# Identity products in TensorE's idle times, and a last stage that scatters its first picks ahead of its second picks

## What is computed

```python
h = _layernorm(x, g, b).reshape(Tn, D)
logits = h @ Wr
top_vals, top_idx = jax.lax.top_k(logits, TOP_K)          # 2 of 7
gates = jax.nn.softmax(top_vals, axis=-1)
idx = top_idx.T.reshape(-1)                               # all first picks, then all second picks
onehot = jax.nn.one_hot(idx, E_ROUTED, dtype=jnp.int32)
pos = jnp.sum(jnp.cumsum(onehot, axis=0) * onehot, axis=-1) - 1
keep = pos < CAPACITY
xe = zeros.at[idx, where(keep, pos, CAPACITY)].set(h[tok], mode='drop')
ye = (silu(xe @ W1) * (xe @ W3)) @ W2
routed = zeros.at[tok].add(ye[idx, pos] * gates * keep)
out = routed + silu(h @ W1s) * (h @ W3s) @ W2s
x = _layernorm(x + out)
```

## Time and profile before

| | us |
|---|---|
| median of 3 runs | 2411.19 |
| fastest, slowest | 2404.15, 2413.72 |
| the profiled execution | 2407.47 |
| its span, first to last instruction | 2405.6 |
| TensorE busy | 2038.5 (85%) |
| VectorE busy | 1331.8 (55%) |
| ScalarE busy | 1129.3 (47%) |
| GpSimd busy | 969.7 (40%) |
| mean granted TensorE clock | 0.906 |

### The profile page before, as it was taken

How to read it: one execution, slowest core, us unless ns; L and a number is a source line. 1 busy time by engine, 2 the same in 40 slices (tenths; PEclk the granted TensorE clock), 3 DMA queues, 4 the chain that set the end, 5 groups by cost and what they waited for, 6 DMA issues and landing times. The chain is left out here.

```text
span 2405.6 us, 59384 instructions
## 1 busy us (share of the span) xinstructions
PE 2038.5 (85%) x24530; PEld 1251.5 (52%) x24530; DVE 1331.8 (55%) x3370; ACT 1129.3 (47%) x2591; POOL 969.7 (40%) x868
## 2 busy tenths in 40 slices
PE   4988999869976899999999999999769756699773
PEld 2445666635543555565555555555535545355452
DVE  3545554447725776767776767776236423465322
ACT  1333445115523676767676767676415211145221
POOL 2010000011215887878787878787110133100123
PEclk8999999879968999999999999999769767889887
DMA  2110000000002021211111212121000032100411
GB/s 66 24 36 1 1 1 1 1 18 3 3 1 72 18 60 27 47 39 42 40 47 35 60 27 51 36 48 24 14 14 7 1 110 89 27 2 2 132 39 40
DMA packets 70558, 78.47 MB, mean 33 GB/s; under 512 B 10608, under 2 KB 48634, under 8 KB 70291
## 3 DMA queue, kind: packets, MB, share of 16 engines
q1 hardware_dynamic: 64098, 61.75, 9.9%
q0 software_dynamic: 3696, 10.56, 1.5%
q10 hardware_dynamic: 2496, 2.36, 0.4%
HBM read 40.90 MB, written 6.82 MB: 20 GB/s over the span
## 5 line engine op out<-in xcount | busy, mean ns | idle before, releaser
L3490 POOL TENSOR_TENSOR l1fb_rinv<-l1fb_ssq,neghalf 128x8 f32<-128x8 f32 x192 | 316.2, 1647 | 159.5 <-DVE l1fb_ssq L3533 157.0
L3633 ACT ACTIVATE l1fb_p<-ps,l1fb_shift 128x64 f32<-128x64 f32 x768 | 177.7, 315 | 158.7 <-PE ps L3789 137.8
L3492 POOL TENSOR_TENSOR l1fb_qk<-l1fb_qk,l1fb_r 128x512 f32<-128x512 f32 x192 | 244.5, 1273 | 0.0
L3696 PE MATMUL ps<-l1fb_wqkv,l1fb_xs 128*128 128x512 f32 x384 | 219.5, 655 | 10.3 <-DVE l1fb_r L3543 6.2
L3494 POOL TENSOR_TENSOR l1fb_qk<-l1fb_qk,l1fb_rinv 128x512 f32<-128x512 f32 x192 | 200.4, 1044 | 15.1
L3543 DVE TENSOR_TENSOR l1fb_r<-ps,l1fb_turn_tab 128x256 f32<-128x256 f32 x384 | 143.0, 414 | 0.0
L3540 DVE TENSOR_TENSOR l1fb_qk<-ps,l1fb_turn_tab 128x512 f32<-128x512 f32 x192 | 132.4, 690 | 14.4 <-POOL l1fb_qk L3492 12.5
L3531 DVE TENSOR_REDUCE l1fb_ssq<-l1fb_sq 128x8 f32<-128x512 f32 x192 | 129.8, 676 | 3.0 <-ACT l1fb_sq L3613 3.0
L3613 ACT ACTIVATE l1fb_sq<-ps 128x512 f32<-128x512 f32 x192 | 118.7, 618 | 11.9 <-PE ps L3696 11.2
L3727 PE MATMUL ps<-ident,l1fb_qk 128*128 128x128 f32 x768 | 116.6, 275 | 5.7 <-POOL l1fb_qk L3494 2.5
L3641 ACT ACTIVATE l1fb_both<-ps 128x512 f32<-128x512 f32 (+1 forms) x194 | 117.3, 605 | 8.3 <-PE ps L3789 7.7
(11 more groups left out here) (722 smaller groups left out, 4773.8 us busy)
## 6 DMA issues: line engine op xcount, KB each, us to landing
l1fb_v<-l1fb_v SPq DMA_DIRECT2D x48, 260.0 KB, 4.2
l1fb_v<-l1fb_v SPq DMA_DIRECT2D x48, 195.0 KB, 4.0
l1fb_wqkv<-in_L_ffn_Wqkv SPq DMA_DIRECT2D x24, 256.0 KB, 2.8
l3f_w<-in_L_ffn_W SPq DMA_DIRECT2D x21, 256.0 KB, 6.5
l1fb_wqkv<-in_L_ffn_Wqkv SPq DMA_DIRECT2D x6, 512.0 KB, 4.7
l1fb_wo<-in_L_ffn_Wo SPq DMA_DIRECT2D x6, 512.0 KB, 4.1
l1fb_w<-in_L_ffn_W SPq DMA_DIRECT2D x6, 341.0 KB, 3.0
l3f_xs<-zeros SPq DMA_DIRECT2D x1, 1344.0 KB, 6.9
```

The costliest lines, as they stand in the source:

```text
L3490: nc.gpsimd.tensor_tensor(w.rinv[:, u, :], w.ssq[:, u, :], chip.neghalf[:, 0:8], ALU.pow).then_inc(*w.unit_norm.end(f"rinv{u}"))
L3492: nc.gpsimd.tensor_tensor(w.qk[:, u, :], w.qk[:, u, :], fp(w.r2), ALU.add).then_inc(*w.unit_norm.end(f"add{u}"))
L3633: last = nc.scalar.activation(w.p[:, c % 2, q, j, :], ps[:, SCORE_BANK + j, q * SEEN:(q + 1) * SEEN], ACT.Exp, bias=w.shift[:, c, j, q:q + 1])
L3696: nc.tensor.matmul(ps[:, PROJ_BANK(u), :], w.xs[:, x.odd, q * P:(q + 1) * P], w.wqkv[:, col:col + 512], start=True, stop=True)\
```

## The change

A helper `stay_busy(nc, chip, bank, n)` issues n products of the bf16 identity with itself, 128x128 by 128x512, into a PSUM bank whose contents nobody needs at that time. Nobody reads them and no semaphore counts them. It is called at 25 places of the list of TensorE, 575 products in all, each time ahead of a wait or at the end of a stage's list:

| stage | place and number of products |
|---|---|
| l0_attn | ahead of the wait for wk 18; ahead of the first slot 24; end 8 |
| l0_xattn | start 19; end 24 |
| l0_ffn | end 6 |
| l1_attn | ahead of the wait for xT0 9; ahead of the first slot 37; ahead of each wait for `gained` 5, 5, 5 and 32; end 7 |
| l1_xattn | end 12 |
| l1_ffn | entry, ahead of the wait for the loads 14; ahead of the wait for the first weights 9; behind the last transposes 44 |
| l2_attn | ahead of the first slot 24; ahead of the first transposed scores 8 (`ahead=8`); end 9 |
| l2_xattn | ahead of the first two waits for `norm` 5 and 5; end 6 |
| l2_ffn | start of the main loop 95; end 80 |
| l3_attn | end 13 |
| l3_xattn | ahead of the first slot 28; end 6 |
| l3_ffn | between the shared expert and expert 1 18 |

In l3_ffn the steps are cut into one half for the first picks and one for the second. The two PSUM banks are opened at the start. hT is made in two halves, one by DVE and one by ACT. TensorE counts after each pick, ahead of the shared expert. A function `placed(s)` gives the places of one half; it adds up the totals in three doubling steps in place of a chain. POOL scatters the eight columns of first picks when `sent0` is there. At the end, DVE adds the shared result to the residual before the gathered rows arrive (`kepty`), works through the batches one by one, and normalises six tiles and then two. SP stores `out` within the same block, in two transfers; the block at the end is gone.

The diff, cut to its core. The calls of `stay_busy` are all of the form shown here:

```diff
+def stay_busy(nc, chip, bank, n):
+
+    for _ in range(n):
+        nc.tensor.matmul(chip.ps[:, bank, :], chip.ident_b[:, :], chip.ident_b[:, :].unsqueeze(1).to_broadcast([P, 4, P]), start=True, stop=True)
...
             def late(kind, b):
                 if kind == "turn":
+                    stay_busy(nc, chip, MISC, 5 if b < B - 1 else 32)
                     eng.wait_ge(*gains.of(b))
...
+            stay_busy(nc, chip, 0, 95)
             turn(0)
...
+            batch = lambda b, n: chip.out[b:b + n, :, :].rearrange("b (t p) d -> p b t d", p=P)
+            sp.wait_ge(*bdve.done("normed"))
+            sp.dma_start(batch(0, B - 1), chip.x_tok[:, 0:B - 1, :, :]).then_inc(written, 16)
+            sp.wait_ge(*bdve.done("normed_last"))
+            sp.dma_start(batch(B - 1, 1), chip.x_tok[:, B - 1:B, :, :]).then_inc(written, 16)
+            sp.wait_ge(written, 32)
...
+            nc.gpsimd.memset(fp(run), 0.0).then_inc(*rpool.end("runs"))
             eng.wait_ge(*emptied.of(0))
-            eng.wait_ge(*cdve.done("sent"))
             for i in range(2 * TILES):
+                if i % TILES == 0:
+                    eng.wait_ge(*cdve.done(f"sent{i // TILES}"))
...
-            for pair in range(B // PAIR):
-                tails_pool(nc, eng, chip, t[PAIR * pair:], dve, pool, pair)
+            early, late = slice(0, TILES - QT), slice(TILES - QT, TILES)
+            for part, which in ((early, ""), (late, "_last")):
+                eng.wait_ge(*bdve.done(f"var{(part.stop - 1) // QT}"))
+                nc.gpsimd.tensor_tensor(yroot[:, part], ymv[:, part, 1], chip.eps[:, part], ALU.add).then_inc(*bpool.end("eps" + which))
+                eng.wait_ge(*bpool.done("eps" + which))
+                nc.gpsimd.tensor_tensor(yroot[:, part], yroot[:, part], chip.neghalf[:, part], ALU.pow).then_inc(*bpool.end("rstd" + which))
...
-            eng.wait_ge(*rpe.done("zT"))
-            nc.vector.tensor_scalar(fp(hT), ps[:, 4:6, :].rearrange("p a t -> p (a t)"), w["L3_ffn_ln_g"], w["L3_ffn_ln_b"],
-                                    ALU.mult, ALU.add).then_inc(*rdve.end("hT"))
+            eng.wait_ge(*rpe.done("zT0"))
+            nc.vector.tensor_scalar(hT[:, 0:512], ps[:, 4, :], w["L3_ffn_ln_g"], w["L3_ffn_ln_b"], ALU.mult, ALU.add).then_inc(*rdve.end("hT0"))
...
+            def placed(s):
+                at = slice(s * TILES, (s + 1) * TILES)
+                bank = (5, 4)[s]
+                n = TILES
+                a0, a1 = run[:, 0, s, :, :], run[:, 1, s, :, :]
+                eng.wait_ge(*cpe.done(f"counts{s}"))
+                eng.wait_ge(*rpool.done("runs"))
+                nc.vector.tensor_copy(a0[:, n + 1:2 * n + 1, :], ps[:, bank, S:S + n * E].rearrange("p (i e) -> p i e", e=E)).then_inc(*cdve.end(f"run{s}"))
+                for src, dst, step, before, name in ((a0, a1, 1, "run", "two"), (a1, a0, 2, "two", "four"), (a0, a1, 4, "four", "eight")):
...
+                    nc.vector.tensor_tensor(dst[:, n:2 * n + 1, :], src[:, n:2 * n + 1, :], src[:, n - step:2 * n + 1 - step, :], ALU.add)\
...
+                nc.vector.tensor_tensor(offs[:, at, :], ps[:, bank, 0:n * E].rearrange("p (i e) -> p i e", e=E), a1[:, n:2 * n, :], ALU.add)\
...
+                    nc.vector.tensor_tensor(offs[:, at, :], offs[:, at, :], run[:, 1, 0, 2 * n:2 * n + 1, :].to_broadcast([P, n, E]), ALU.add)\
...
+                nc.vector.scalar_tensor_tensor(offs[:, at, :], offs[:, at, :], float(L3_CAPACITY - 1), w["c_slots"][:, 0:E].unsqueeze(1)
...
+                nc.vector.tensor_scalar(sent[:, at], away[:, at], w["c_slots"][:, E:E + 1], None, ALU.add).then_inc(*cdve.end(f"sent{s}"))
+
+            placed(0)
             mixed(0)
-            eng.wait_ge(*cpe.done("counts"))
-            totals = ps[:, 5, S:S + 2 * TILES * E].rearrange("p (i e) -> p i e", e=E)
-            for i in range(1, 2 * TILES):
...
-                nc.vector.tensor_tensor(offs[:, i, :], offs[:, i - 1, :], totals[:, i - 1, :], ALU.add).then_inc(*cdve.end(f"off{i}"))
-                if i == TILES:
-                    mixed(1)
...
+            placed(1)
+            mixed(1)
...
+            nc.vector.tensor_tensor(fp(kepty), ps[:, 6:8, :].rearrange("p a (t d) -> p (a t) d", d=D), x_tiles, ALU.add).then_inc(*bdve.end("kept"))
             eng.wait_ge(*cdve.done("weight"))
-            for pair in range(B // PAIR):
-                for b in range(PAIR * pair, PAIR * pair + PAIR):
-                    eng.wait_ge(*gathered[b].of(2 * QT - 1))
...
-                tails_dve(nc, eng, chip, t[PAIR * pair:], dve, pool, pair, lambda i: bdve.done(f"both{PAIR * pair + i}"),
-                          lambda i: mixedy[:, (PAIR * pair + i) * QT:(PAIR * pair + i + 1) * QT, :], lambda i: chip.x_tok[:, PAIR * pair + i, :, :])
+            eng.wait_ge(*bdve.done("kept"))
+            for b in range(B):
+                tiles = range(b * QT, b * QT + QT)
+                eng.wait_ge(*gathered[b].of(2 * QT - 1))
...
+            for which, part in (("", range(0, TILES - QT)), ("_last", range(TILES - QT, TILES))):
+                eng.wait_ge(*bpool.done("rstd" + which))
+                for q in part:
+                    last = nc.vector.tensor_scalar(x_tiles[:, q, :], mixedy[:, q, :], ymv[:, q, 0:1], yroot[:, q:q + 1], ALU.subtract, ALU.mult)
+                last.then_inc(*bdve.end("normed" + which))
...
+            eng.wait_ge(*rpe.done("zT1"))
+            nc.scalar.activation(hT[:, 512:T], ps[:, 5, :], ACT.Identity, bias=w["L3_ffn_ln_b"], scale=w["L3_ffn_ln_g"]).then_inc(*ract.end("hT1"))
...
+            for half in range(2):
+                nc.tensor.matmul(ps[:, 6 + half, :], chip.zeros[0:1, 0:P], chip.ones[0:1, 0:512], start=True, stop=False)
             eng.wait_ge(*rdve.done("z"))
+            for half in range(2):
+                for q in range(4):
+                    last = nc.tensor.transpose(ps[:, 4 + half, q * P:(q + 1) * P], z[:, 4 * half + q, :], chip.ident[:, :])
+                last.then_inc(*rpe.end(f"zT{half}"))
...
+                if q == 0:
+                    eng.wait_ge(*rdve.done("hT0"))
+                if q == 4:
+                    eng.wait_ge(*ract.done("hT1"))
                 last = nc.tensor.matmul(ps[:, 4, q * E:(q + 1) * E], hT[:, q * P:(q + 1) * P], w["L3_ffn_Wr"], start=True, stop=True)
...
-            for half in range(2):
-                nc.tensor.matmul(ps[:, 6 + half, :], chip.zeros[0:1, 0:P], chip.ones[0:1, 0:512], start=True, stop=False)
...
+            for s, pick in enumerate(("firstpick", "secondpick")):
+                eng.wait_ge(*rdve.done(pick))
+                if s == 0:
+                    eng.wait_ge(*ract.done("hT1"))
+                flat = picks[:, s * TILES:(s + 1) * TILES, :].rearrange("p i e -> p (i e)")
+                nc.tensor.matmul(ps[:, (5, 4)[s], 0:TILES * E], w["c_before"], flat, start=True, stop=True)
+                nc.tensor.matmul(ps[:, (5, 4)[s], S:S + TILES * E], chip.ones[:, 0:P], flat, start=True, stop=True).then_inc(*cpe.end(f"counts{s}"))
...
+                    eng.wait_ge(*cdve.done("pos1"))
...
                 if g == first(1):
+                    eng.wait_ge(*cdve.done("pos1"))
+                    stay_busy(nc, chip, 4, 18)
                     turn(1)
...
-                if g == 0:
-                    counts()
```

More of the change, by code:

```diff
@@ L2905, in l3_ffn @@
         gathered = [counted(chip, f"gathered{b}", 16) for b in range(B)]
-        rpe = lasting(chip, "scores", ["zT", "logits"])
-        rdve = lasting(chip, "maxima", ["stats", "var", "z", "hT", "logits"] + pick_steps("first") + ["m1", "rest"]
-                     + pick_steps("second") + ["gap", "den", "gate1", "gates"])
-        ract, rpool = stepped(chip, "first_act", ["exp"]), stepped(chip, "first_pool", ["eps", "rstd"])
-        cpe = stepped(chip, "first_pe", ["counts"])
-        cdve = stepped(chip, "first_dve", ["off0"] + [f"off{i}" for i in range(1, 2 * TILES)]
-                     + ["pos", "keep", "row", "mine", "slot", "kept", "home", "away", "sent", "weight"])
+        rpe = lasting(chip, "scores", ["zT0", "zT1", "logits"])
+        rdve = lasting(chip, "maxima", ["stats", "var", "z", "hT0", "logits"] + pick_steps("first") + ["m1", "rest"]
+                       + pick_steps("second") + ["gap", "den", "gate1", "gates"])
+        ract, rpool = stepped(chip, "first_act", ["hT1", "exp"]), stepped(chip, "first_pool", ["eps", "rstd", "runs"])
+        cpe = stepped(chip, "first_pe", ["counts0", "counts1"])
+        places = ["run", "two", "four", "eight", "pos", "keep", "row", "mine", "slot", "kept", "home", "away", "sent"]
+        cdve = stepped(chip, "first_dve", [f"{s}0" for s in places] + [f"{s}1" for s in places[:5] + ["based"] + places[5:]] + ["weight"])
         work = [(0, c, half) for c in range(C) for half in range(2)] + [(r, c, 0) for r in range(1, E + 1) for c in range(C)]
```

127 lines of the change are left out of this document (75 added, 52 removed).

## The result

The changed kernel takes 2346.8 us (median of four runs, 2345.3 to 2351.3), the kernel before 2412.3 us beside it: a ratio of 0.973, 95% interval 0.971 to 0.975, or 65 us less. The forecast was 2350 us. The profiled execution took 2345.65 us.

The account below looks back on a forecast made before the run. Work behind TensorE's holes was taken to run at half clock, the holes bound by other engines or transfers. Clock 47, first picks 9.3 and end 4.0 sum to 60 us off 2407.5: median near 2350 us, range 2322 to 2386.

Parts of the forecast that it names:

- Clock: Work behind filled holes, 23 stretches: identity products keep TensorE's clock up, giving back 47 us, from 17 to 72.
- share of 0.55 of the ceiling: Part of the 85 us clock ceiling expected to come, the middle between bounds 0.2 and 0.85: 47 us.
- 11.1 us at the end of l1_attn: Largest single clock term: last batch of l1_attn, 25.48 us, against 14.33 us for l2_attn's same pattern at full clock.
- Price of a product: All fills: an identity product costs 0.22 us at full clock and 0.43 us at half, nothing while it ends before the wait.
- Between 1 and 2.5 us: At every filled hole: the part the chosen number of products leaves empty at full clock.
- the prediction's own sign of being wrong: At the fills: identity products end behind their wait, TensorE restarting without idle, or the clock is 0.50 right behind them.
- First picks early: l3_ffn: first picks' places come earlier, so scatters and expert 1 start 9.3 us earlier, from 7 to 10.
- End: Closing of l3_ffn: one batch of sums after the last gather and an immediate store save 4.0 us, from 2 to 5.
- Sum: Whole kernel: 47 + 9.3 + 4.0 = 60 us off the profiled execution's 2407.5 us; median near 2350 us.
- signs named in advance: Mean clock 0.95 or more; l1_attn's last batch under 16 us; `l1a_k` scores 1.13 us; expert 1 about 28.5 us; prompt store.
- the holes left open still let the clock fall: Rival: unfilled holes of about 2 us still drop the clock; 20 us clock gain, about 2375 us; chance 0.20.
- identity products do not hold the clock: Rival: identity products count as no work, everything stays at half clock and fills overrun; 2464 us; chance 0.06.

Follow-up runs that it names:

- e1: Changed kernel with every identity product of the change left out, last stage as changed: 2396.0 us, ratio 0.993.
- e2: Kernel before with the identity products at the 24 places outside the last stage; l3_ffn and the store as they were: 2368.3 us, ratio 0.981.
- e8: Changed kernel with one store of the whole output in a block of its own behind the last stage, as before the change: 2350.6 us, ratio 0.976.
- e4: Changed kernel with the first scatter waiting for the places of the second picks too: 2359.3 us, ratio 0.978.
- e3: Changed kernel without the 5 products ahead of the third turn in l1_attn, every other one kept: 2360.4 us, ratio 0.978.
- e9: Changed kernel with 431 of its 575 products on 32 rows of the array in place of 128: 2416.5 us, ratio 1.003.
- e11: Changed kernel with fills lengthened as in e10, plus products at four more places (753 products): 2327.3 us, ratio 0.965.
- e6: Changed kernel with twice as many identity products at every place: 2403.8 us, ratio 0.998.
- e7: Changed kernel with both operands of every such product a tile of zeros in place of the identity: 2350.5 us, ratio 0.976.
- e12: Changed kernel with 431 of its 575 products on all 128 rows but only 32 columns of the array: 2360.5 us, ratio 0.979.
- e10: Changed kernel with each fill longer by the idle time left behind it less 0.4 us (720 products): 2335.0 us, ratio 0.968.

## Why the prediction held, step by step

- **Clock, 47 us (17 to 72):** 46.7 us by the traces (44.6 ahead of l3_ffn, 2.1 in its experts), 47 us by e1, 46 us by e2, which has no fill in l3_ffn. The share of 0.55 of the ceiling was a middle between bounds and no measurement, so its exactness is luck. Single executions with the same code start l3_ffn up to 10 us apart (2210.6 us in e8, 2220.9 us in e4), so the agreement of the traces within a microsecond is luck too. The part that rested on a row was right (11.1 us at the end of l1_attn, confirmed by e3), but not for the reason given. The prediction says that the clock did not come back there because the work is sparse; its own row has TensorE busy 24.83 of 25.48 us. It is dense, and of a kind that doesn't raise the clock (e3, e9). The Trainium skill ("TensorE: Matmul & The Clock Gate", Part 1: The HAM clock gate) has the ramp penalty at under 1% of a typical kernel's span. The runs differ from it here: 1.9% of the span was given back, and e11 gave some 0.8% more.
- **Price of a product:** 0.23 us measured (0.22). "Between 1 and 2.5 us" left of every hole was too tidy: 0 to 2.8 us were left, and one fill, in l2_attn, cost about 0.9 us because it had no hole to fill. That is the prediction's own sign of being wrong, at one place of the 25. The cost of an overrun was right at half clock (40.71 us for 95, e9) and too high in e6's expectation, most likely because longer fills paid part of themselves back in clock.
- **First picks early, 9.3 us (7 to 10):** 10.0 us, at the upper bound. `sent0` came 2.9 us behind the second pick, not 3.5. (The 11.1 us that the prediction names for the old steps are 11.4 by its two times, which its sum uses.) TensorE's slack ahead of expert 1 was 0.88 us (about 1). Of the 10.0 us the order of the scatters is worth 6.1 (e4).
- **End, 4.0 us (2 to 5):** 5.1 us, just over the bound. The block boundary gave its 2.3 us (e8), DVE's and POOL's chain 2.3 (1.7), and 0.5 us came because the store's last part takes 3.05 us and not 3.6: most of the output had left 0.5 us earlier.
- **Sum:** 60 us forecast, 61.8 us between the spans, 65 us (60 to 70) by the medians.
- **Of the signs named in advance** four showed (mean clock 0.960, last batch 14.4 us at 1.00, 27.8 us behind the second pick, store issued at once) and one did not: the score products behind `l1a_k` are still at half clock. That is the rival "the holes left open still let the clock fall", true at several places of about 2 us and false at the one that mattered. Its price is at most what e11 gained, 19 us, of which the traces place 13.7 us at fills that e11 adds, and not the 25 us between it and my forecast. Its condition is also too narrow: in l3_xattn the clock fell with no hole over 0.46 us.
- **The rival "identity products do not hold the clock"** was wrong for this kernel, and its reason was aimed at the wrong property. Values made no difference (e7). Rows did (e9, e12): with 431 of the fills on 32 rows the change gains nothing at all. I argued against it with identity products of 128 rows in the strip stages, which happened to be the right evidence.

## What to carry to other kernels

Fill a wait of TensorE up to within half a microsecond of its end: half a fill bought 8 of 47 us here, and two holes of about 2 us left open cost about 8 us in l2_xattn (e11). Look for the hole in a trace first: a fill without one is paid for (0.9 us in l2_attn). Put a fill first ahead of work that can't bring the clock back by itself, since there one microsecond of products saved twelve (e3). Let the products span all rows of the array, and read the clock, not the busy time, to see whether they work.

## What the runs showed of the hardware

- Products on 32 rows of the array, one after another and without a gap, let the granted clock fall and did not bring it back: 0.50 over 40.64 us and over 28 us (e9). Products on 128 rows and 32 columns ran at 0.97 (e12). Score products on 32 rows that run four at a time are another case: in the changed kernel nothing else ran from 2073.96 to 2077.40 us, at 0.50, and the clock was 0.99 in the next 2 us.
- The last batch of l1_attn, 32-row scores and 128-row value products in turn, stays at the clock at which it starts: 14.38 us at 1.00 in the changed kernel, 26.75 us at 0.50 with TensorE 98% busy in e3. The first slots of l3_xattn do not: there the clock falls in some executions, 28 us behind the first score products (the changed kernel, e4) or 35 us (e7, e8), with no hole over 0.46 us ahead of it in the changed kernel, and in others (e10, e11) not at all.
- Products of zeros hold the clock as those of identities do (mean 0.956 and 0.960).
- Open: what makes the clock fall in the first slots of l3_xattn in one execution and not in another, the rest of the differences of up to 10 us ahead of l3_ffn, and e12's two standstills of ACT and DVE.
